# Head outputs placed transposed by transfers, inverse of the sums on ScalarE, product on GpSimd

## The chip, the core and the metric

The kernel runs on one core of a Trainium2 chip. The metric is device time in microseconds, the median of several executions. The engines are TensorE (PE, with its weight loads as PEld), VectorE (DVE), ScalarE (ACT), GpSimd (POOL) and SyncE (SP), which here only issues transfers. Each engine works off its own queue in the order written; semaphores tie the queues together.

## What is computed

Two decoder layers over x, 16 batches of 256 tokens and 256 channels in float32, with a context of the same shape. Every sublayer is followed by a normalisation without parameters:

```python
x = _layernorm(x + _L0_attn_ref(x, ...))            # 16 heads of 16, rope
x = _layernorm(x + _L0_xattn_ref(x, ctx, ctx, ...)) # gated linear mixing, 8 heads of 32
x = _layernorm(x + _L0_ffn_ref(x, ...))             # quantised, relu^2 * up
x = _layernorm(x + _L1_attn_ref(x, ...))            # 16 heads of 16
x = _layernorm(x + _L1_xattn_ref(x, ctx, ctx, ...)) # 16 heads of 16, keys from ctx
x = _layernorm(x + _L1_ffn_ref(x, ...))
```

In the three attentions with 16 heads, which are all that matters here:

```python
attn = softmax(q @ k.T / 4)            # 256 x 256 for each head
out = attn @ v                         # 256 x 16 for each head, the heads side by side
return out @ w_proj + b_proj
```

## The kernel before

**Lanes.** Four batches are in work at a time, one in each lane, and each lane does four batches one after the other (`it` 0 to 3). A lane has its own tiles: XO (the stream and a second half, `outputs`), YX (two halves: Y, and XT_ which is also OT), QK, V, PB, U. `lane_steps` lists the steps of one batch, `PARTS` says which engines take part in each. `TURNS` holds for each engine a string of digits: the lane whose next step that engine takes. This is a merge of the four lanes, written out by hand or by a planner, and it is the order of each queue. `PLACES` gives each use of psum its first bank of eight.

**One attention.** The steps are xT (transpose of the stream), qk (projection, split into two halves of 16 bits, written to DRAM by SyncE), stack (read back with head pairs on partitions), v, then eight steps max (scores of one pair of heads on TensorE L767, row maxima on VectorE L1170), negmax (the maxima as a further row of Q), eight steps exp (scores again L786, exponential on ScalarE L1005) and between them four steps pv.

**From pv to proj.** A pv step (L804) multiplies with weights of 32 columns out of V. V keeps for each head 16 values and a column of ones, 17 columns side by side, so that a head's 32 rows in psum hold 16 numerators, the sum of the exponentials, and rows that nobody needs. ScalarE copies psum to U in two pieces of 128 x 512 (L1009). The step heads turns U by eight transposes into two psum banks (L817), VectorE takes the reciprocal of the 32 sums of each token (L1181) and multiplies into `outputs` (L1183). The step oT turns this back by four transposes (L681, through `turn_x`), ScalarE copies to OT (L1012), and proj multiplies OT by W_o (L694, through `tokens_out`). VectorE then adds the stream (L1189), and moments and norm follow (L1100, L1103, L958, L960, L1111). GpSimd has the rope sums (L1342), the bias for the stream (L1347) and two products in mixout (L1357, L1361).

**Order around it.** K of the third attention is projected and stored while the second runs: its copy on ScalarE goes into U and so waits for `o_ready` of the second (L985). `loadx` waits for oT of the third attention (L638). The first heads step of each batch waits for the store of the batch before, which reads the same half of XO (L1180).

Of the kernel before, what the change touches and what calls it, by code (L numbers as in the profile page):

```python
# [12 lines left out]
ALU = mybir.AluOpType  # L13
# [3 lines left out]
P = 128  # L17
LANES = 4
# [10 lines left out]
SLOT = 32  # L29
# [15 lines left out]
    "exp": "pe act", "pv": "pe act", "heads": "pe dve", "oT": "pe act", "proj": "pe dve act", "norm": "dve",  # L45
# [7 lines left out]
WIDTH = {"ctx": 1, "xT": 1, "rope": 1, "qk": 1, "v": 1, "max": 2, "negmax": 1, "exp": 2, "pv": 1, "heads": 2, "oT": 1,  # L53
# [4 lines left out]
def lane_steps():  # L58
# [6 lines left out]
    def attention(a):  # L65
# [15 lines left out]
        add("pv", a, 3)  # L81
        add("heads", a)
# [4 lines left out]
        add("oT", a)  # L87
# [57 lines left out]
def lane_program(lane):  # L145
# [7 lines left out]
    for at in range(-1, batches):  # L153
# [10 lines left out]
        "0010002102210131223113433220000000000011011110010100322001203202101202211103111230103112020133000001"  # L164
        "2001003102202213213222121321111120331120110021200233301332330222223322032230101321131100021103030310"
        "1013333302322103323320300120230100012011001021120032332133001130321230110212112312121332132111132332"
        "1322233212213222302300022220331323330032031211033311310001332223301223002002021021103223011201221211"
        "0212021323213330200000120200101200001333211130010331211113003332303322300311032113200323112223111230"
        "0002100120133100230320301110333011210211103331120212203012001033122002310102212022133201133223121123"
        "1112333210330130320331023300322022322303010121112203223010201203130003301331121232033233220031000231"  # L170
        "0000120011011100001202111232033031113111321123221322111122313330210001202233302220322303220233200122"
        "2201123001002033210030133310333103123202230333301113000032220311101121021130012220122210222010123231"
        "1212123031211110332111320023000223301333312333122033122300230103200230101230100132220130111030331021"
        "1011233330000322133211301002100120012230322032213231331222321211132123301000231102033323302102212313"
        "3201303032322220320120030031313331331100103310232312211210032320002010010100110111000020232333021330"
        "1121321112311221110231022111120013022300220122102223223320002222111200100030211323300110301320211210"
        "3111233130233310000033211333122312333130130013030022002221322322111223311233011121033212300111203320"
        "0323330222331233311222031112030110000320003002230303033303332033331220211312201112011231000110031032"
        "1031001220332221022133122223121111123311211023101002203303332033320223222131101310221322101232330103"
        "0131033313020200023232033221003230001000102110012011220130331331100130321131121221312232213111131023"  # L180
        "3032132212233232223022013211022223133112333113332100233113011033332213110112011232100231000021002012"
        "0033202210220322223022312333121321233301333203332330323032321320233330330"),
    "act": (
        "0012000311242211332000000000301003011011110110121010221000002010122201022122220311111120331022021233"
        "3003333122210233221300101321130123213311123333221033203002200300300200023230231203011330110310111113"
        "3131211312221222122122232222333332332320333300033310000003121113002320121221102212211022100200000120"
        "0200110123111133211133333332232313120103022233230000002203310030301111033013101110331110002300122122"
        "1012102221211220021311023333023033120332330031221202230101302112033211221333312311221033220030002000"
        "0002033000123110123203203111111131313111333132112222222220222022020300200203320330033033313303033310"
        "1130000130311111211001222022212220012102211112121112112232323313332333303220300023220000330200310311"  # L190
        "0130313011011303030011331310020122220122021201122221130211303202330112332003322203313013100322132322"
        "1303213331312313021212111030223000030000000023022302330132011113111131113111123212231222012222232000"
        "2220002000220001011113110333301130300003311333132313313300300122022212222021112112111231122333212333"
        "2223333320230000003220003020320033333003333310111011103111100110020122120221202122120232111103311203"
        "1202103213303320333122232101032120110323123320131323311222330220300020030023000032221303130110331011"
        "1111331133111320102122122222222322223333323332133231131333111113011131003000010002001202221220222022"
        "122311113303322333333330032232202310203333330"),
    "dve": (
        "0012210004321344311220000000044111111141223223202220033300330010031010033011020112112002210121201121"
        "3200013100232120100302302123013123321313132112313132010233000223232202223323111333131333130002022012"  # L200
        "0200112111113222332232223300330333120012200001033030001110000011113212213312112111222122030302203333"
        "2202231300331130011330333010120100212010221010321113003211220000321230002010222111332332113121113103"
        "1203030302223032222213232211133310000103330030333312211222112111022220303333222302003011100030320332"
        "1121330111300000011112212231223113211222200022033033222333001300133103033033113201002210022101201113"
        "0002131232102000233021332100202113321123321131111110312330002220330222322302021211001031000331332221"
        "1121231313231130322202022223313330031100000330333301112331020021110001012112121123112332220003332332"
        "2320223022330033130013130033101101200112210101212112020311223030122132300102023213000020213312312311"
        "3113131302203302023223222220331311133133013333001102122111211200200333223023222132213130330033332221"
        "33311222333000"),
    "pool": (  # L210
        "0022211033030032110112210320113332230000110302223111220330012231313102122003331122333010022000111102"
        "22300113330113322221003203311313022000211111122003232223330001112030023213133332233110122203"),
    "sp": (
        "4220011300002121110224443313332443000011110221223333201100011322202313233001200000312110111222223133"
# [92 lines left out]
def decoder_kernel(nc, x, ctx, consts, w_qkv0, w_proj0, w_gates, b_gates, w_gate, w_up, w_down,  # L307
# [3 lines left out]
    with es:  # L311
# [167 lines left out]
        def freed_by(it, name, L, occ, unit, j):  # L479
# [22 lines left out]
            if name == "heads":  # L502
                return [(o_ready[L], a + 1)]
# [896 lines left out]
```

## Time and profile before

| what | value |
|---|---|
| median of 3 runs | 1617.05 us (1615.44 to 1617.6) |
| profiled execution, its own time | 1622.2 us |
| its span | 1620.4 us |
| busy: PE, DVE, ACT, POOL | 1465.2, 1183.2, 950.7, 225.4 us |
| granted TensorE clock, mean | 0.969 |
| largest group on DVE | row maxima, 384 x 1223 ns |
| largest group on ACT | exponentials, 384 x about 1025 ns |

Busy time of an engine is the union of its instructions. TensorE's matmuls are pipelined, so the duration of one (some 280 to 400 ns) is longer than the pace at which they follow each other. Idle time of an engine is put down to what ended it.

### The profile page before, as it was taken

What the parts mean: (1) busy time and instruction counts of PE and PEld (TensorE: products, weight loads), DVE (VectorE), ACT (ScalarE), POOL (GpSimd) and SP (SyncE); (2) the same over time, 40 slices, a digit from 0 to 9 for tenths busy, and PEclk for the clock granted to TensorE, in tenths of its full rate; (3) what the DMA queues carried; (4) which work ended last, traced back from release to release, by engine and by line L of the source; (5) the groups of instructions that cost most, each with busy time, mean ns of one, the idle gap of its engine ahead of it and who ended that gap; (6) DMA issues with size and microseconds to landing.
All of it is one profiled execution on the core that took longest, in us unless ns stands there. A gap on an engine that the chain in (4) does not pass through costs nothing. (4 is left out here: it accounts for less than half of the span.)

```text
span 1620.4 us, 31692 instructions
## 1 busy us (share of the span) xinstructions
PE 1465.2 (90%) x12482; PEld 972.9 (60%) x12482; DVE 1183.2 (73%) x2103; ACT 950.7 (59%) x1701; POOL 225.4 (14%) x233
## 2 busy tenths in 40 slices
PE   7588799899999879899999888998999988898998
PEld 4155556557766556557767555565776656465577
DVE  5978887865568888974765888866565788888632
ACT  3378466674466757566355666656545586655752
POOL 6011100002221011002212210000122111100100
PEclk9699989999999999999999898999999999999999
DMA  8430113322121021521321011331322101133200
GB/s 273 139 102 2 52 47 105 118 60 79 53 69 51 2 63 48 152 67 58 119 73 53 1 47 33 93 108 50 111 72 66 53 2 46 47 97 110 70 1 26
DMA packets 115074, 114.34 MB, mean 71 GB/s; under 512 B 9842, under 2 KB 100722, under 8 KB 114930
## 3 DMA queue, kind: packets, MB, share of 16 engines
q1 hardware_dynamic: 114610, 111.28, 22.4%
q8 instruction: 102, 1.67, 0.4%
q10 hardware_dynamic: 320, 1.05, 0.3%
q14 instruction: 42, 0.34, 0.1%
HBM read 68.91 MB, written 42.99 MB: 69 GB/s over the span
## 5 line engine op out<-in xcount | busy, mean ns | idle before, releaser
L1170 DVE TENSOR_REDUCE nm<-psum 128x4 f16<-128x1024 f32 x384 | 455.1, 1223 | 100.3 <-PE psum L767 99.2
L1005 ACT ACTIVATE PB<-psum 128x1024 f32<-128x1024 f32 x288 | 288.3, 1024 | 87.1 <-PE psum L786 85.7
L804 PE MATMUL psum<-PB,V 128*32 128x256 f32 x2304 | 206.8, 390 | 7.4 <-ACT PB L1005 5.2
L1347 POOL TENSOR_TENSOR XO<-XO,row_b 128x512 f32<-128x512 f32 x80 | 103.2, 1300 | 749.8 <-ACT YX L976 749.8
L767 PE MATMUL psum<-QK 48*128 48x256 f16 x1536 | 140.4, 280 | 46.8 <-DVE nm L1170 22.7
L786 PE MATMUL psum<-QK 49*128 49x256 f16 x1536 | 138.3, 277 | 21.4 <-ACT PB L1005 5.3
L767 PEld LDWEIGHTS psum<-QK 48*128 48x128 f16 x1536 | 58.9, 96 | 109.8 <-DVE nm L1170 38.8
L786 PEld LDWEIGHTS psum<-QK 49*128 49x128 f16 x1536 | 54.2, 95 | 111.4 <-issue 42.1
L930 PE MATMUL psum<-YX,W 128*128 128x256 f32 x512 | 120.0, 385 | 0.0
L804 PEld LDWEIGHTS psum<-PB,V 128*32 128x32 f32 x2304 | 79.9, 110 | 62.6 <-issue 20.0
L938 PE MATMUL psum<-W,PB 128*128 128x256 f32 x512 | 116.3, 382 | 0.0
L1005 ACT ACTIVATE YX<-psum 128x1024 f32<-128x1024 f32 x96 | 98.7, 1028 | 20.3 <-PE psum L786 20.0
L804 PE MATMUL psum<-YX,V 128*32 128x256 f32 x768 | 101.3, 385 | 5.1 <-ACT PB L1005 4.9
L930 PEld LDWEIGHTS psum<-YX,W 128*128 128x128 f32 x512 | 94.4, 190 | 17.3 <-issue 4.2
L938 PEld LDWEIGHTS psum<-W,PB 128*128 128x128 f32 x512 | 95.8, 190 | 13.9 <-issue 1.7
L694 PE MATMUL psum<-W_o,YX 128*128 128x256 f32 x384 | 97.8, 401 | 1.1 <-ACT YX L1012 0.5
L1111 DVE TENSOR_SCALAR XO<-YX,mv,rstd 128x256 f32<-128x256 f32 x192 | 79.5, 457 | 24.6 <-ACT rstd L960 24.3
L1009 ACT ACTIVATE U<-psum 128x512 f32<-128x512 f32 x112 | 66.9, 599 | 50.6 <-PE psum L804 43.3
L681 PE MATMUL psum<-cst,XO 128*128 128x128 f32 x512 | 81.8, 283 | 13.3 <-DMA XO<-in_x 4.2
L694 PEld LDWEIGHTS psum<-W_o,YX 128*128 128x128 f32 x384 | 73.1, 199 | 16.1 <-issue 2.6
L681 PEld LDWEIGHTS psum<-cst,XO 128*128 128x128 f32 x512 | 58.4, 142 | 38.9 <-issue 16.3
L1189 DVE TENSOR_TENSOR YX<-psum,XO 128x512 f32<-128x512 f32 x48 | 33.0, 688 | 64.3 <-PE psum L694 44.4
(171 smaller groups left out, 2675.4 us busy)
## 6 DMA issues: line engine op xcount, KB each, us to landing
QK<-heads_dram SPq DMA_DIRECT2D x96, 512.0 KB, 3.8
heads_dram<-U SPq DMA_DIRECT2D x288, 128.0 KB, 2.0
XO<-in_x SPq DMA_DIRECT2D x16, 256.0 KB, 3.2
YX<-in_ctx SPq DMA_DIRECT2D x16, 256.0 KB, 3.4
out<-XO SPq DMA_DIRECT2D x16, 256.0 KB, 2.5
W<-in_w SPq DMA_DIRECT2D x2, 1024.0 KB, 6.9
heads_dram<-PB ACTq DMA_DIRECT2D x4, 256.0 KB, 9.4
W_gu<-in_w_down SPq DMA_DIRECT2D x1, 1024.0 KB, 5.6
```

The lines of the kernel that those rows point to most:

```text
L681: ins = pe.transpose(bank[:, k * TOK + t * P:k * TOK + t * P + P], src[:, t, k * P:(k + 1) * P], ident)
L694: ins = pe.matmul(bank[:, t * DIM:(t + 1) * DIM], xt(k)[:, t * P:(t + 1) * P], w[:, k], start=(k == 0), stop=(k == n - 1))
L767: ins = pe.matmul(b[:, e * 512 + t * TOK:e * 512 + (t + 1) * TOK], QS[L][r, unit, t * P:(t + 1) * P], KS[L][r, unit, :], start=True, stop= ...
L786: ins = pe.matmul(b[:, e * 512 + t * TOK:e * 512 + (t + 1) * TOK], KS[L][r, unit, t * P:(t + 1) * P], QS[L][r, unit, :], start=True, stop= ...
L804: ins = pe.matmul(b[SLOT * j:SLOT * j + SLOT, at:at + TOK], value(L, t, PAIRS * e + u, HEADS, HD, SLOT), src, start=(t == 0), stop=(t == T ...
L930: ins = pe.matmul(b[:, m * TOK:(m + 1) * TOK], W_1[:, k, c:c + P], XT_[L][:, k, :], start=(k == 0), stop=(k == KT - 1))
L938: ins = pe.matmul(b[:, 0:DIM], hid1(L, k)[:, unit * P:(unit + 1) * P], W_2[:, k], start=(k == 0), stop=(k == IT - 1))
L1005: act.activation(weights_of(L, unit), b[:, 0:1024], ACT.Exp, scale=HD ** -0.5)\
L1009: act.activation(flat2(U[L][:, unit - 1:unit + 1, :]), b[:, 0:512], ACT.Copy).then_inc(u_ready[L], 1)
L1111: dve.tensor_scalar(stream(L, it)[:, t], Y[L][:, t], mv[L][:, t, 0:1], rstd[L][:, t:t + 1], ALU.subtract, ALU.mult).then_inc(x_ready[L], 1)
L1170: dve.tensor_reduce(nm[L][:, :, :, unit].rearrange("p t e -> p e t"), b[:, 0:1024].rearrange("p (e t k) -> p e t k", e=2, t=TT), AX.X, ALU ...
L1347: pool.tensor_tensor(stream(L, it), stream(L, it), row_b[:, occ:occ + 1, :].to_broadcast([P, TT, DIM]), ALU.add).then_inc(xb_ready[L], 1)
```

## The change

V becomes `[P, 1024]`: each head has 32 columns in which value and one alternate, so numerators come on even rows and copies of the sum on odd rows, 16 of each a head. The steps heads (of TensorE and VectorE) and oT disappear. A new step spread issues four transfers on SyncE after the second copy to U: even rows of two groups of U to OT, odd rows to `sums`, which is the Y half of YX, each transfer 64 partitions by 2 x 256. The step heads is now Ln and Exp with scale -1 on ScalarE over `sums`, in place, and a product of OT and `sums` in place on GpSimd. Then proj, as before.

```diff
-    "exp": "pe act", "pv": "pe act", "heads": "pe dve", "oT": "pe act", "proj": "pe dve act", "norm": "dve",
+    "exp": "pe act", "pv": "pe act", "spread": "sp", "heads": "act pool", "proj": "pe dve act", "norm": "dve",
...
-        V = lanes("V", [P, TT * HEADS * (HD + 1) + SLOT])
+        V = lanes("V", [P, TT * HEADS * 2 * HD])
...
+        sums = [v[:, 0].rearrange("p (k t) -> p k t", k=KT) for v in YX]
+        VA, ones = ([v[:, :].rearrange("p (n d c) -> p n d c", d=HD, c=2)[:, :, :, n] for v in V] for n in range(2))
...
+        def value(lane, t, e, u):
+            at = (t * HEADS + PAIRS * e + u) * 2 * HD
+            return V[lane][:, at:at + 2 * HD]
...
                 elif name == "loadx" and it:
-                    sp.wait_ge(turned[L], nth(TURNED, it - 1, "oT2"))
+                    sp.wait_ge(turned[L], nth(TURNED, it - 1, "quant"))
...
+                elif name == "spread":
+                    sp.wait_ge(u_ready[L], it * U_USES + U_AT[occ] + 2)
+                    for home, other in ((OT, 0), (sums, 1)):
+                        for g in range(2):
+                            sp.dma_start(home[L][64 * g:64 * g + 64, :, :], U[L][other:P:2, g:4:2, :])\
+                              .then_inc(spread[L], 16)
...
-                elif name == "oT":
-                    b = claim(*step)
-                    pe.wait_ge(o_ready[L], it * ATTN + occ + 1)
-                    filled(turn_x(outputs(L, it), b), *step)
                 elif name == "proj":
...
-                    pe.wait_ge(turned[L], nth(TURNED, it, f"oT{occ}"))
+                    pe.wait_ge(o_ready[L], it * ATTN + occ + 1)
...
                         if unit:
-                            act.wait_ge(o_ready[L], it * ATTN + 2)
+                            act.wait_ge(spread[L], (it * ATTN + 2) * 64)
...
-                elif name == "oT":
-                    b = wait_full(act, *step)
-                    act.activation(flat2(OT[L][:, :, :]), b[:, 0:512], ACT.Copy).then_inc(turned[L], 1)
+                elif name == "heads":
+                    act.wait_ge(spread[L], (it * ATTN + occ + 1) * 64)
+                    log = own(act.activation(flat2(sums[L][:, :, :]), flat2(sums[L][:, :, :]), ACT.Ln))
+                    wait_own(log)
+                    act.activation(flat2(sums[L][:, :, :]), flat2(sums[L][:, :, :]), ACT.Exp, scale=-1.0)\
+                       .then_inc(inverse_ready[L], 1)
...
-                    inverse = own(dve.reciprocal(sums, b[:, :, HD]))
-                    wait_own(inverse)
-                    dve.tensor_tensor(outputs(L, it).rearrange("p t (h d) -> p (t h) d", d=HD), b[:, :, 0:HD],
-                                      sums.rearrange("p (h d) -> p h d", d=1).to_broadcast([P, TT * HEADS, HD]),
-                                      ALU.mult).then_inc(o_ready[L], 1)
...
+                elif name == "heads":
+                    pool.wait_ge(inverse_ready[L], it * ATTN + occ + 1)
+                    pool.tensor_tensor(flat2(OT[L][:, :, :]), flat2(OT[L][:, :, :]), flat2(sums[L][:, :, :]), ALU.mult)\
+                        .then_inc(o_ready[L], 1)
```

The wait for the store of the batch before moves to mixnorm on ScalarE, the first writer of `outputs` that is left. The memsets of V become memsets of its columns of ones, once a lane at the start, and half of them again before the second attention. The small tiles aT, eneg, den, vr, q_s, h_s and q_k share one tile. `TURNS` and `PLACES` are new throughout: TensorE has 1777 steps in place of 1873, ScalarE 1345 as before, VectorE 966 (1014), GpSimd 240 (192), SyncE 342 (294).

## Rows read from the trace of the kernel before

**Rows 1.** The page, busy time of each engine, share of the span, instructions.
```profile
PE 1465.2 (90%) x12482; PEld 972.9 (60%) x12482; DVE 1183.2 (73%) x2103; ACT 950.7 (59%) x1701; POOL 225.4 (14%) x233
```
**Rows 2.** Stretches of 100 us: length, busy of each engine, clock, transfers.
```profile
core 0: us, PE busy (x) PEld busy (x) DVE busy (x) ACT busy (x) POOL busy (x), PEclk, DMA share, GB/s
...
400.00:500.00 100.00, 99.28 (x759) 69.72 (x757) 61.14 (x99) 53.83 (x98) 19.93 (x18) 1.00 0.23 71
500.00:600.00 100.00, 83.54 (x777) 52.85 (x776) 87.05 (x180) 66.38 (x136) 12.79 (x13) 0.93 0.06 20
...
900.00:1000.00 100.00, 83.98 (x706) 53.77 (x704) 84.23 (x176) 61.57 (x133) 16.23 (x16) 0.88 0.07 20
```
**Rows 3.** Who waited for whom: us in total, times, longest.
```profile
PEld psum L767 <- DVE nm L1170: 38.8, 53, 5.4
...
PEld psum L804 <- ACT PB L1005: 23.9, 48, 1.2
...
PEld psum L786 <- ACT PB L1005: 21.3, 42, 1.6
...
PEld psum L767 <- ACT PB L1005: 12.0, 22, 2.1
```
**Rows 4.** Groups by line and form: count, busy us, mean ns, idle before, releaser.
```profile
L681 PE MATMUL psum<-cst,XO 128*128 128x128 f32 x512 | 81.8, 283 | 13.3 <-DMA XO<-in_x 4.2 <-DVE XO L1183 3.9 <-DVE XO L1111 2.7
...
L817 PE MATMUL psum<-cst,U 128*128 128x128 f32 x448 | 61.7, 279 | 3.8 <-DVE nm L1170 1.8 <-ACT U L1009 1.4 <-ACT YX L976 0.3
...
L1183 DVE TENSOR_TENSOR XO<-psum,rs 128x512 f32<-128x512 f32 x48 | 33.2, 691 | 1.7
...
L1012 ACT ACTIVATE YX<-psum 128x512 f32<-128x512 f32 x48 | 28.7, 600 | 40.0 <-PE psum L681 39.9
...
L1181 DVE RECIPROCAL rs<-psum 128x32 f32<-128x32 f32 x48 | 16.9, 352 | 41.1 <-PE psum L817 40.9
```
**Rows 5.** Instructions in order of time, 1570 to 1577 us: start, us.
```profile
1570.69 1.07 PE L804 MATMUL psum<-PB,V 128*32 128x256 f32 x16
...
1573.53 1.04 PE L817 MATMUL psum<-cst,U 128*128 128x128 f32 x8
...
1574.40 1.89 PE L930 MATMUL psum<-YX,W 128*128 128x256 f32 x8
...
1576.13 0.60 PE L681 MATMUL psum<-cst,XO 128*128 128x128 f32 x4
...
1576.56 1.89 PE L930 MATMUL psum<-YX,W 128*128 128x256 f32 x8
```
**Rows 6.** Instructions on heads_dram: ns to issue (min/median/max), then landing of 128 KB.
```profile
L644 SPq DMA_DIRECT2D heads_dram<-U x192: 354/470/3081, 21.6 to 1522.9; - x192
...
DMA to landing us min/median/max: 1.8/2.1/12.0
```
**Rows 7.** Landing of the 512 KB reads of line L653; the page's queue line.
```profile
DMA to landing us min/median/max: 3.1/3.8/6.7
...
q1 hardware_dynamic: 114610, 111.28, 22.4%
```
**Rows 8.** Groups by line and form, for the prices of added instructions.
```profile
L1347 POOL TENSOR_TENSOR XO<-XO,row_b 128x512 f32<-128x512 f32 x80 | 103.2, 1300 | 749.8 <-ACT YX L976 749.8
...
L1009 ACT ACTIVATE U<-psum 128x512 f32<-128x512 f32 x112 | 66.9, 599 | 50.6 <-PE psum L804 43.3 <-PE psum L887 6.8
...
L1072 ACT ACTIVATE PB<-PB 128x1024 f32<-128x1024 f32 x32 | 33.8, 1057 | 1.0
```
**Rows 9.** VectorE and GpSimd in order of time near 555 us; line L1111, ns.
```profile
554.65 2.93 DVE L1111 TENSOR_SCALAR XO<-YX,mv,rstd 128x256 f32<-128x256 f32 x2
...
554.71 1.26 POOL L1357 TENSOR_TENSOR XO<-YX,row_b 128x512 f32<-128x512 f32 x1 [15.03 <-DVE YX L1256]
556.10 1.26 POOL L1361 TENSOR_TENSOR YX<-XO 128x512 f32<-128x512 f32 x1
...
L1111 DVE TENSOR_SCALAR XO<-YX,mv,rstd x192: 380/407/1564, 90.9 to 1617.4; 128x256 f32<-128x256 f32 x192
```
**Rows 10.** Groups by line and form, for the prices of TensorE's steps.
```profile
L767 PE MATMUL psum<-QK 48*128 48x256 f16 x1536 | 140.4, 280 | 46.8 <-DVE nm L1170 22.7 <-DVE U L1153 6.6 <-DMA QK<-heads_dram 5.5
...
L938 PE MATMUL psum<-W,PB 128*128 128x256 f32 x512 | 116.3, 382 | 0.0
```

More of the change, by code:

```diff
@@ L51 @@
 }
-WIDTH = {"ctx": 1, "xT": 1, "rope": 1, "qk": 1, "v": 1, "max": 2, "negmax": 1, "exp": 2, "pv": 1, "heads": 2, "oT": 1,
+WIDTH = {"ctx": 1, "xT": 1, "rope": 1, "qk": 1, "v": 1, "max": 2, "negmax": 1, "exp": 2, "pv": 1,
          "proj": 1, "gates": 1, "vm": 1, "turn": 1, "decay": 2, "mix": 2, "mixv": 1, "mixnorm": 1, "quant": 1, "gate": 2, "up": 2,
@@ L81, in attention @@
         add("pv", a, 3)
+        add("spread", a)
         add("heads", a)
@@ L238 @@
+    "03536036153560526043642604306406310474163452707505227610615425024"
 )
@@ L373, in decoder_kernel @@
         nmT = [v[64:64 + HEADS, 0:TOK // 2].bitcast(F16) for v in GN]
-        rs = lanes("rs", [P, TT, HEADS])
         st = lanes("st", [P, TT, 6])
@@ L379, in decoder_kernel @@
         M3 = lanes("M3", [P, TOK], BF16)
-        aT = lanes("aT", [P, TT, MH])
-        eneg = lanes("eneg", [P, TT, MH])
-        den = lanes("den", [P, TT * MH])
-        vr = lanes("vr", [P, TT * MH])
-        q_s = lanes("q_s", [P, TT, 4])
-        h_s = lanes("h_s", [P, TT, 6])
-        q_k = lanes("q_k", [P, TT, 3])
+        small = lanes("small", [P, 4, TT * MH])
+        aT, eneg = ([v[:, n].rearrange("p (t h) -> p t h", t=TT) for v in small] for n in range(2))
+        den, vr = ([v[:, n] for v in small] for n in (2, 3))
+        q_s, h_s, q_k = ([v[:, 0:2].rearrange("p n c -> p (n c)")[:, at:at + TT * n].rearrange("p (t n) -> p t n", t=TT) for v in small]
+                         for at, n in ((0, 4), (8, 6), (20, 3)))
         heads_dram = [nc.dram_tensor(f"heads_dram{i}", [2, 2, 4, HD, PAIRS, TOK], F16, kind="Internal").ap()
@@ L406, in decoder_kernel @@
         o_ready, y_ready, moments, x_ready = (lane_sem(n) for n in ("o_ready", "y_ready", "moments", "x_ready"))
+        spread, inverse_ready = lane_sem("spread"), lane_sem("inverse_ready")
         mix_dve, quantized = lane_sem("mix_dve"), lane_sem("quantized")
@@ L458, in weights_of @@
             return YX[lane][:, :, :].rearrange("p a n -> p (a n)") if u % SLOTS == PBUF else PB[lane][:, u % SLOTS, :]
-        def value(lane, t, h, heads, width, columns):
-            at = (t * heads + h) * (width + 1)
-            return V[lane][:, at:at + columns]
+        def value(lane, t, e, u):
+            at = (t * HEADS + PAIRS * e + u) * 2 * HD
+            return V[lane][:, at:at + 2 * HD]
         def decays(lane, h, n):
@@ L501, in freed_by @@
                 return [(u_ready[L], it * U_USES + U_AT[occ] + unit // 2 + 1)]
-            if name == "heads":
-                return [(o_ready[L], a + 1)]
-            if name == "oT":
-                return [(turned[L], nth(TURNED, it, f"oT{occ}"))]
             if name == "proj":
@@ L1322, in _ @@
             for L in range(LANES):
-                setup(pool.memset(V[L][:, :], 0.0))
-            pool.wait_ge(set_pool, 4 + LANES)
-            for L in range(LANES):
-                setup(pool.memset(VA[L][:, :, :, HD:HD + 1], 1.0))
+                setup(pool.memset(ones[L], 1.0))
             setup(pool.memset(ones_sq, 1.0))
```

171 lines of the change are left out of this document (81 added, 90 removed).

## The prediction

> **What bounds the kernel now.** I read the busy shares first, then the table by stretches of 100 us, then who waits for whom. TensorE is busy 1465.2 us of 1620.4, VectorE 1183.2, ScalarE 950.7, GpSimd 225.4 [rows 1]. A share of 90% is an average: in six of the sixteen stretches TensorE is busy 94 to 99 us of 100 (300 to 500, 700 to 900, 1100 to 1300), and nothing but its own work can shorten these. In 0 to 200, 500 to 600, 900 to 1000 and 1300 to 1400 it is at 66 to 87 while VectorE mostly stands at 84 to 90 [rows 2]: there the row maxima set the pace. The waits say the same: TensorE's weight loads wait for the maxima to free a bank (38.8 us) and for the exponentials of ScalarE (23.9, 21.3 and 12.0 us) [rows 3]. So: TensorE first, VectorE second, ScalarE in short waits. The granted clock is 1.00 in the full stretches and 0.88 to 0.93 in the two thin ones shown, both far nearer the 2.4 GHz level than 1.2.
>
> **What the change removes.** There are 48 attentions (16 batches, 3 each). Each loses eight transposes of U (step heads), one reciprocal and one 128x512 product on VectorE, four transposes (step oT) and one 128x512 copy on ScalarE. TensorE: the transposes of U are 448 instructions in 61.7 us, of which 384 belong to attentions: 52.9 us; those of XO are 512 in 81.8 us, 192 of them oT: 30.7 us; together 83.6 us [rows 4]. This is the upper bound, since a group's busy time holds a modelled tail that overlaps the next group. The lower bound comes from starts: eight transposes begin at 1573.53 and the next matmuls at 1574.40, four begin at 1576.13 and the next at 1576.56, so 0.87 + 0.43 = 1.30 us an attention, 62.4 us in all [rows 5]. I take the middle, 73 us. VectorE loses 16.9 + 33.2 = 50.1 us, ScalarE 28.7 us [rows 4]. The two psum banks of heads and one of oT are also no longer claimed; no wait names them alone, so nothing is booked.
>
> **What it adds.** The weighted sums keep their 32 columns, now values and ones alternating, so their matmuls cost the same. SyncE issues four transfers of 128 KB, ScalarE runs Ln and Exp over 128x512 in SBUF, GpSimd one 128x512 product. A transfer of 128 KB takes 0.47 us to issue and lands 2.1 us after its issue [rows 6]; one of 512 KB lands in 3.8 [rows 7]. An activation over 1024 SBUF columns takes 1.057 us and one over 512 from psum 0.599, so I price each of the two at 0.60; the nearest GpSimd product takes 1.30 on average [rows 8], and 1.26 undisturbed [rows 9]. ScalarE: 48 x 1.20 - 28.7 = +28.9 us; GpSimd +62 us, on an engine 14% busy; transfers +25 MB on a queue that holds the 16 DMA engines for 22.4% of the span with 111 MB [rows 7]: +5 points. SyncE: 192 more issues, 90 us, on a queue that mostly waits; behind a spread step stand most often a qk step (20 of 48) and a negmax (8), which it can hold for its 1.9 us of issuing, or longer when the last pair of U is late.
>
> **Where it lies.** The new chain from the last weighted sum to proj is 0.60 (copy to U) + 4 x 0.47 + 2.1 (last landing) + 1.20 + 1.27 + six hand-overs of about 0.1 = 7.65 us. The old one was 0.60 + 0.87 + 0.36 + 0.69 + 0.43 + 0.60 + 0.6 = 4.2 us. So each attention takes 3.5 us longer in its lane, and the question is whether TensorE's written order covers it, because its queue stops at proj until o_ready. I expanded the new order: between the last pv step and proj of the same attention stand 4 to 20 steps of other work, 11.3 on average (before, 5 to 19 and 11.5, of which two were heads and oT). Priced by step (a max or exp step 140.4 / 384 = 0.37 us, a down1 step 116.3 / 32 = 3.6 [rows 10], a pv step 1.07 and a projection about 1.9 [rows 5], and so on) and stretched so that the whole order fills 1565 us, these gaps are 5.5 us at least and 9.3 in the middle. Eight of the 48 are under 7.65, short by 4.5 us together. If the chain were 10 us, 31 would be short by 49 us; at 12 us 36 by 118. The same limit stands for ScalarE: it waits for the transfers at the head of its queue with exp steps behind it (in the new order 13 times at once), and its U copy of another lane too.
>
> **The sum.** Relief of TensorE 73. Charged back: (a) in 5 of 16 stretches VectorE sets the pace and its relief is 50, so (73 - 50) x 5/16 = 7; (b) late proj steps 4.5; (c) VectorE and GpSimd disturb each other. Beside two GpSimd products a pair of normalising instructions took 2.93 us [rows 9], where one such takes 0.380 at least and two 0.73. There are 96 such pairs; a further 48 products with a window of 2.0 us each meet 96 x 48 x 2.0 / 1570 = 6 of them at some 1.2 us: 7 us with both sides' delays, bounds 0 and 61 (every product holds VectorE for its 1.27 us); (d) ScalarE goes from 58.7% to 62% busy, so its queueing (share over the rest) grows by a sixth, and the 57.2 us that loads wait for it [rows 3] by 10. Total 28.5; gain 44.5. The profiled execution took 1622.2 us, its span 1620.4: 1622.2 - 44.5 = 1577.7. The median of the runs, 1617.05, lies 5.15 below, so 1572.5; I say 1572. The new merges and bank places were drawn up afresh for all engines: no row prices that; the nearest is TensorE's idle 155 us, of which a tenth either way, 15 us, goes into the range and nothing into the value. The start and the end: the first memsets and the last down1 steps keep their kind and count; 0.
>
> On (c), the Trainium skill (SBUF — State Buffer, Who interferes with whom) says that a VectorE instruction with two SBUF inputs, or in a two-port mode, and a GpSimd instruction that reads SBUF lock each other out for a whole instruction. By that rule the trace agrees in kind [rows 9], and by it the change moves work into the lock.
>
> On the transfers, the Trainium skill (DMA: Bandwidth & Descriptors, Rules for kernel authors) says of two transfers to disjoint halves of the partitions that they serialize, since both use all 16 DMA engines, and advises one; here there are four of 64 partitions. By that, four times 2.1 us would make a chain of about 12 us. The trace speaks against it so far: of 288 transfers of 128 KB, issued in twos and threes less than half a microsecond apart, the median lands in 2.1 us [rows 6].
>
> **Rivals.** (1) *The relief counts only where TensorE is full.* Elsewhere it turns into longer waits for the maxima and for lanes that got 3.5 us longer. Then 6/16 x 73 = 27 less charges of about 10: 1617 - 17 = 1600. For it: the waits [rows 3]. Against: VectorE is relieved by 50 too. (2) *The upper bound holds*: 83.6 and hardly a charge, the longer chain wholly under other lanes' work: 1535. For it: gaps of 9.3 against 7.65. (3) *Slower: the transfers land late.* The place is the proj step at the head of TensorE's queue. It decides from a chain of 10 us, a last landing of 4.5 us in place of 2.1, since the 49 us short then eat the gain. At 12 us, 118 - 4.5 = 113.5; half of it is won back because the other lanes are then readier: 1572 + 57 = 1629. For it: landings up to 12.0 and 6.7 us [rows 6, 7], and stacks of 512 KB in the same stretches. Against: the medians. (4) *The lock holds VectorE for every product*: 61 instead of 7: 1626. Against: most VectorE time is maxima with one psum input. (5) *No effect within 0.2%*: the charges meet the relief, 1617.
>
> **How the numbers follow.** Forecast, 1550 to 1592: 0.56. Rival 1: 0.17. Rival 2: 0.10. Rival 3: 0.09. Rival 4: 0.03. Rival 5: 0.05. Faster by over 0.2% (below 1613.8) 0.56 + 0.17 + 0.10 = 0.83; within 0.2%, about what a measurement of this kernel tells from no change, 0.05; slower 0.12. The range: below, relief 83.6 with no charge and a few us of better merging, 1530; above, rival 1 with its own spread, 1607. Left out are rivals 3 to 5 and the edges, just under 0.2.
>
> **What the profile after would show.** TensorE near 1390 us busy with 576 transposes fewer and idle near 185; VectorE about 1133 to 1140; ScalarE about 980; GpSimd near 287; the four transfers landing at 2 to 2.5 us; waits of the proj matmuls for GpSimd under 10 us; normalising pairs beside GpSimd products in some 15 places. Wrong would be: landings over 4.5 us, proj waits of tens of us, idle time of TensorE grown by more than 60 us (then rival 1 or 3), a ScalarE activation from SBUF over 0.7 us, or a TensorE clock well under the 0.97 of the span.

## The result and the profile after

The changed kernel takes 1661.7 us in the median (1656.4 to 1667.6), beside 1617.3 us for the kernel before (1615.4 to 1620.0): a ratio of 1.027 [1.023, 1.031]. It is slower by 44 us where 45 faster was forecast, and 55 us above the end of the range. The profiled execution has a span of 1662.0 us and a mean granted clock of 0.949, against 1620.4 and 0.969 before.

The busy line of the page, which answers to [rows 1]:

```profile
PE 1438.5 (87%) x11886; PEld 930.7 (56%) x11906; DVE 1139.1 (69%) x2007; ACT 979.4 (59%) x1749; POOL 288.5 (17%) x277
```

All three helpers came out as forecast (VectorE 1133 to 1140, ScalarE 980, GpSimd 287). TensorE did not (near 1390 was forecast): its 576 transposes are gone, yet it is busy only 27 us less, and its idle time (span less busy) rose from 155 to 223 us. So the time came as idle time of TensorE. A part of the small 27 is the clock: busy time times granted clock is 1420 before and 1365 after, 55 us less work, and the lower clock stretches what is left. (That product is a fair measure of TensorE's work here: four more kernels below run the same 12482 instructions as the kernel before, and it is 1418 to 1421 for them.)

Who waited for whom, from all of the run (engine, line, what it waited for: us, times, longest), which answers to [rows 3]:

```profile
ACT YX L1006 <- DMA YX<-U: 96.0, 41, 5.5
...
PEld psum L767 <- DVE nm L1172: 38.3, 52, 3.0
...
PEld psum L786 <- ACT PB L999: 26.5, 38, 2.2
...
PEld psum L804 <- ACT PB L999: 25.1, 40, 1.6
...
PEld psum L694 <- issue: 22.5, 39, 2.5
...
PE psum L694 <- POOL YX L1331: 19.6, 15, 3.1
```

The old waits stand nearly where they stood. New are the first and the last: ScalarE stands at Ln for the transfers in 41 of 48 attentions, 96 us in all, and TensorE stands at proj (L694) for GpSimd's product. The weight loads of proj wait 22.5 us where they waited 4.9 before. From the single instructions, proj starts within 0.2 us of the end of the product in 19 of 48 attentions.

One attention in order of time (start us, us, engine, line, operation, tiles; in brackets the idle time before it and what ended it):

```profile
1145.99 0.60 ACT L1003 ACTIVATE U<-psum 128x512 f32<-128x512 f32 x1 [1.19 <-PE psum L804]
...
1146.62 3.32 SPq L653 DMA_DIRECT2D YX<-U  x4
...
1152.63 0.63 ACT L1006 ACTIVATE YX<-YX 128x512 f32<-128x512 f32 x1 [1.89 <-DMA YX<-U]
...
1153.29 0.63 ACT L1008 ACTIVATE YX<-YX 128x512 f32<-128x512 f32 x1
...
1153.83 1.01 ACT L999 ACTIVATE PB<-psum 128x1024 f32<-128x1024 f32 x1
1154.00 1.26 POOL L1331 TENSOR_TENSOR YX<-YX 128x512 f32<-128x512 f32 x1 [2.43 <-ACT YX L1008]
...
1155.38 2.07 PEld L694 LDWEIGHTS psum<-W_o,YX 128*128 128x128 f32 x8 [2.07 <-issue]
1155.41 2.76 PE L694 MATMUL psum<-W_o,YX 128*128 128x256 f32 x8 [1.82 <-POOL YX L1331]
```

Here the whole mechanism stands in a few lines. The copy to U begins at 1145.99 and the product ends at 1155.26, 9.3 us later; ScalarE stands idle for 1.89 us with an exp (1153.83) behind it, TensorE for 1.82 us with other lanes' steps behind proj. Over the 48 attentions that stretch, from the start of the last U copy to the end of the product, is 8.7 us at least and 8.9 in the middle; the prediction said 7.65.

The rows of the transfers (ns to issue, least/median/most; then the landing), which answer to [rows 6]:

```profile
L653 SPq DMA_DIRECT2D YX<-U x192: 593/607/2047, 76.0 to 1624.2; - x192
...
DMA to landing us min/median/max: 2.9/3.4/4.6
```

Groups by line, which answer to [rows 8]:

```profile
L1331 POOL TENSOR_TENSOR YX<-YX 128x512 f32<-128x512 f32 x48 | 62.0, 1291 | 668.9 <-ACT YX L1008 668.8
...
L1006 ACT ACTIVATE YX<-YX 128x512 f32<-128x512 f32 x48 | 30.2, 630 | 96.0 <-DMA YX<-U 96.0
```

And the three stretches of [rows 2] (columns as there):

```profile
400.00:500.00 100.00, 93.56 (x701) 63.98 (x694) 60.03 (x94) 51.05 (x90) 24.76 (x22) 1.00 0.28 75
500.00:600.00 100.00, 81.52 (x788) 50.81 (x787) 82.53 (x158) 70.75 (x143) 16.16 (x14) 0.95 0.18 51
900.00:1000.00 100.00, 86.83 (x816) 53.82 (x818) 78.94 (x164) 73.38 (x147) 13.42 (x13) 0.95 0.20 54
```

The stretch that was full, 99.28 us of 100, now has holes, though with the whole kernel running late it no longer holds quite the same work. That is the opposite of relief.

### The profile page after: what moved, and what is told of

It is laid out like the page before. It is cut to its first block and busy times, and to the rows that moved or that the text cites. A ratio compares the mean times of both kernels' runs of the same rounds, so it can differ in the third digit from the quotient of the medians.

```text
span 1662.0 us, 30607 instructions
## 1 busy us (share of the span) xinstructions
PE 1438.5 (87%) x11886; PEld 930.7 (56%) x11906; DVE 1139.1 (69%) x2007; ACT 979.4 (59%) x1749; POOL 288.5 (17%) x277
## 2 busy tenths in 40 slices
DMA packets 142719, 139.46 MB, mean 84 GB/s; under 512 B 12914, under 2 KB 128370, under 8 KB 142578
## 5 line engine op out<-in xcount | busy, mean ns | idle before, releaser
L999 ACT ACTIVATE PB<-psum 128x1024 f32<-128x1024 f32 x288 | 287.7, 1024 | 103.5 <-PE psum L786 102.3
L804 PE MATMUL psum<-PB,V 128*32 128x256 f32 x2304 | 214.8, 403 | 14.5 <-ACT PB L999 9.9
L1331 POOL TENSOR_TENSOR YX<-YX 128x512 f32<-128x512 f32 x48 | 62.0, 1291 | 668.9 <-ACT YX L1008 668.8
L786 PE MATMUL psum<-QK 49*128 49x256 f16 x1536 | 143.4, 283 | 33.7 <-ACT PB L999 13.4
L694 PE MATMUL psum<-W_o,YX 128*128 128x256 f32 x384 | 106.6, 426 | 23.8 <-POOL YX L1331 19.6
L804 PE MATMUL psum<-YX,V 128*32 128x256 f32 x768 | 104.8, 395 | 4.0 <-ACT PB L999 4.0
L694 PEld LDWEIGHTS psum<-W_o,YX 128*128 128x128 f32 x384 | 77.5, 211 | 43.2 <-issue 16.1
L1006 ACT ACTIVATE YX<-YX 128x512 f32<-128x512 f32 x48 | 30.2, 630 | 96.0 <-DMA YX<-U 96.0
```

The costliest lines, as they stand in the source:

```text
L694: ins = pe.matmul(bank[:, t * DIM:(t + 1) * DIM], xt(k)[:, t * P:(t + 1) * P], w[:, k], start=(k == 0), stop=(k == n - 1))
L786: ins = pe.matmul(b[:, e * 512 + t * TOK:e * 512 + (t + 1) * TOK], KS[L][r, unit, t * P:(t + 1) * P], QS[L][r, unit, :], start=True, stop= ...
L804: ins = pe.matmul(b[SLOT * j:SLOT * j + SLOT, at:at + TOK], value(L, t, e, u), src, start=(t == 0), stop=(t == TT - 1))
L999: act.activation(weights_of(L, unit), b[:, 0:1024], ACT.Exp, scale=HD ** -0.5)\
L1331: pool.tensor_tensor(flat2(OT[L][:, :, :]), flat2(OT[L][:, :, :]), flat2(sums[L][:, :, :]), ALU.mult)\
```

## The experiments

Times are medians beside the kernel before on the same chip; where two experiments are compared, I take the difference of their ratios times 1617. The theory from the profile after: the transfers make the chain longer than the new orders allow, and each late proj is passed on to every queue. Against it: the order is at fault, ScalarE's stall, or the lock of VectorE.

**old_order: the new flow in the old order.** The orders of before with heads and oT struck, and the new steps put in their places.

> The new data flow (transfers, inverse on ScalarE, product on GpSimd) in the old merge: the order and bank places of the kernel before, with heads and oT struck out of TensorE's and VectorE's queues, ScalarE's new step where oT stood, spread and the GpSimd product put in where the trace of before has their inputs ready. Theory T1 (the chain from the last weighted sums to proj is 8.9 us instead of 7.65 and stalls TensorE at proj): the old order leaves less other work in that gap than the new one, so it is no faster than the changed kernel, 1660 to 1720 us. Theory T2 (the newly drawn merge and bank places cost what the relief gives): 1560 to 1590 us.

Measured: 1795.3 us, ratio 1.109 [1.105, 1.113]. That is slower than the 1660 to 1720 expected. Two waits at proj (L699), and two of ScalarE for the transfers, in all of the run:

```profile
PEld psum L699 <- issue: 99.3, 44, 8.5
...
PE psum L699 <- POOL YX L1336: 95.0, 38, 8.3
...
ACT U L987 <- DMA YX<-U: 60.0, 14, 6.1
...
ACT YX L1011 <- DMA YX<-U: 49.4, 18, 5.9
```

The place of the wait is proj, as the theory says. But the kernel differs from the changed one in two more ways. ScalarE's new step stands in oT's place, a choice of mine. And the copy of K for the third attention (L987) now stands ahead of that step and waits for the transfers itself, 60 us in all, where the changed kernel waits at Ln alone. So the 176 us are no measure of the old order itself.

**no_transfer: what the transfers cost.** SyncE issues none; ScalarE copies U to both homes.

```diff
-  ... sp.dma_start(home[L][64*g:64*g+64, :, :], U[L][other:P:2, g:4:2, :])
-  log = own(act.activation(flat2(sums...), flat2(sums...), ACT.Ln))
-  act.activation(flat2(sums...), flat2(sums...), ACT.Exp, scale=-1.0)
+  log = own(act.activation(flat2(sums...), flat2(U[L][:, 2:4, :]), ACT.Copy))
+  act.activation(flat2(OT...), flat2(U[L][:, 0:2, :]), ACT.Copy)
```

> The changed kernel without its 192 transfers: ScalarE copies two groups of U to sums and two to OT (two instructions of 128x512, as many as Ln and Exp), so the product works on unplaced data. Left out: the placing and the inverse. The chain loses 4 issues and the landing, 5.5 of 8.9 us. T1: TensorE's idle 224 us falls by 60 or more, 1570 to 1600 us. T2: the order is unchanged, so 1640 to 1660 us.

Measured: 1608.3 us, 0.993 [0.990, 0.995]. Without transfers the change is a small gain; 56 us of loss come with them. But even so the gain is 12 us, not 44: part of the forecast fell for another reason.

**old_no_transfer: the same in the old order.**

> The new data flow without transfers (two copies of 128x512 on ScalarE in their place, the copies of the second attention taken from CT; the placing and the inverse are left out) in the order and bank places of the kernel before, less heads and oT. Beside no_transfer (1608 us, the same flow in the new order) it is the price of the order. If the new order is worth less than the old one once the chain is short, this one is at 1550 to 1575 us. If the removed transposes are simply worth little (the time is held by VectorE, the lanes and the clock), it is within 10 us of 1608.

Measured: 1689.5 us, 1.042 [1.039, 1.045]. Neither of the two outcomes expected came. It is again far above its twin in the new order, again with ScalarE's step in oT's place. The transfers cost 108 us in the old order and 56 in the new. That the new order absorbs a part of them is likely but not shown: some of the 108 are the waits of K's copy.

**sums_first: only the sums hold up ScalarE.** The sums' two transfers are issued first and have their own semaphore; GpSimd waits for the numerators. It computes the same as the changed kernel.

```diff
-  for home, other in ((OT, 0), (sums, 1)):
+  for home, other, done in ((sums, 1, spread_sums), (OT, 0, spread)):
...
-  act.wait_ge(spread[L], (it * ATTN + occ + 1) * 64)
+  act.wait_ge(spread_sums[L], (it * ATTN + occ + 1) * 32)
...
+  pool.wait_ge(spread[L], (it * ATTN + occ + 1) * 32)
```

> The changed kernel with the two transfers of the sums issued first and counted on a semaphore of their own, so that Ln and Exp run while the numerators land: the chain is 1.3 us shorter, all work is the same. T1: 48 late steps of which about 18 are late by it: 10 to 30 us faster than the changed kernel, 1632 to 1652 us. T2: within 5 us of it.

Measured: 1617.7 us, 0.999 [0.997, 1.001]. The waits that changed:

```profile
ACT YX L1006 <- DMA YX<-U: 41.6, 23, 3.9
...
PE psum L693 <- POOL YX L1332: 5.5, 8, 1.5
```

Ln and Exp now run beside the numerators' landing. The chain falls from 8.9 to 7.8 us in the middle (from 8.7 to 7.4 at least), and the whole loss goes: 46 us for 1.1 to 1.3 us of chain in 48 attentions, twice what was expected.

**whole_rows: the step in the source.** The source is 64 neighbouring partitions instead of every second one; bytes, packets and issues are the same.

```diff
-  U[L][other:P:2, g:4:2, :]
+  U[L][64 * other:64 * other + 64, g:4:2, :]
```

> The changed kernel with each transfer taking 64 neighbouring rows of U in place of every second row, same bytes and packets; Ln and Exp are copies here, since numerators land in sums. Left out: the right placing and the inverse. If the step of two rows is what makes a landing 3.5 us instead of 2.1, it falls to 2.1 and the time by 15 to 30 us. If the landing is set by four transfers of 64 partitions one behind another, it stays at 3.3 to 3.5 and the time within 5 us of the changed kernel.

Measured: 1629.4 us, 1.006 [1.004, 1.008]. Its transfers:

```profile
L653 SPq DMA_DIRECT2D YX<-U x192: 590/609/1886, 78.7 to 1597.6; - x192
...
DMA to landing us min/median/max: 2.4/2.4/4.1
```

The landing is 2.4 us in place of 3.4, the issue as before, and the kernel gains 35 us. Each of the four, issued 0.6 us apart, lands after 2.4 us, so they don't stretch one another here; with the step the first takes 3.0 in the middle and the last 3.5. What makes 3.4 is which partitions are read: every second one of 128, not 64 neighbours. Ln and Exp are copies in this kernel, but they take 0.630 us each as before.

**first_and_whole: both.**

> sums_first and whole_rows together: sums issued first with their own semaphore, each transfer from 64 neighbouring rows (landing 2.4 us instead of 3.5); Ln and Exp are copies, the placing and the inverse are left out. The chain is 6.4 us, against 7.5 in sums_first, 7.7 in whole_rows and 3.3 in no_transfer. If the gain saturates once the chain is under the gaps of the written order: 1606 to 1614, as without any transfer. If each microsecond of chain is worth the same throughout: about 1590.

Measured: 1609.2 us, 0.994 [0.991, 0.996]: as no_transfer, though all the transfers are there. Their load on the DMA engines costs nothing that can be told from the noise here (2 us, with intervals of 4 either way); what costs is their latency.

The chain of all these, and of the next two experiments, with least and median over the 48 attentions, worked out from single instructions of the traces (start of the last U copy to the end of the product; in the kernel before, to the end of the copy to OT):

| kernel | least | median | ratio |
|---|---|---|---|
| kernel before | 4.3 | 7.2 | 1 |
| no_transfer | 3.2 | 7.2 | 0.993 |
| act_free | 7.1 | 7.3 | 0.996 |
| first_and_whole | 6.4 | 7.6 | 0.994 |
| sums_first | 7.4 | 7.8 | 0.999 |
| whole_rows | 7.6 | 8.4 | 1.006 |
| tuned | 7.4 | 8.4 | 1.014 |
| changed kernel | 8.7 | 8.9 | 1.027 |

Down to a median of 7.6 or so a shorter chain is worth something; below it ScalarE isn't at the step yet (median 7.2 where 3.2 would do), and nothing more comes. The first row matters as much. The old chain could take 4.3 us, but in the middle it took 7.2, because its steps stood in the queues waiting for their turn. So up to about 7.2 us the new chain replaces waiting that was there already, and only the rest is late.

**act_free: is it ScalarE's stall?** ScalarE does five small activations in place of Ln and Exp and never waits for the transfers; GpSimd does.

```diff
-  act.wait_ge(spread[L], ...)
-  ... Ln, Exp
+  for n in range(5): ... act.activation(spare, ident[:, 0:16], ACT.Copy)
...
-  pool.wait_ge(inverse_ready[L], ...)
+  pool.wait_ge(spread[L], ...)
```

> The changed kernel with ScalarE not waiting for the transfers: in its step heads it runs five small copies on a spare tile (about 1.2 us as before), and GpSimd multiplies as soon as the transfers have landed. Left out: the inverse. The chain is 1.3 us shorter, as in sums_first (1617 us), but ScalarE's 96 us of waiting at that step are gone wholly, where sums_first keeps 42. If only the length of the chain counts: 1612 to 1622. If ScalarE's stall with exponentials queued behind it is a cause of its own: 1595 to 1610.

Measured: 1615.7 us, 0.996 [0.993, 0.999], overlapping sums_first. With ScalarE's wait at this step wholly gone, the gain over sums_first is 5 us, within the noise, and no more than the still shorter chain (7.3 for 7.8 us) would give. The stall acts as a part of the chain; a cost of its own doesn't show.

**tuned: ScalarE's step later.** sums_first, with ScalarE's step moved one to three steps back in 14 places, behind steps of other lanes, and proj in 4.

> sums_first with 15 or so of ScalarE's heads steps moved behind one to three steps of other lanes, where they waited over 0.5 us for the transfers, and five proj steps moved behind one step of TensorE. Same work. If ScalarE's stalls are a cause: 5 to 15 us faster than sums_first, 1603 to 1612. If not: within 4 us of it, or slower since the inverse comes later.

Measured: 1642.9 us, 1.014 [1.008, 1.020], 25 us worse than sums_first. Moving the wait away from the head of ScalarE's queue moves the inverse, and with it proj, later: the chain is 8.4 us in the middle for 7.8. Here such local moves did harm even though the moved step had waited.

**struck_old and struck_new: what the removed work is worth.** In both, heads and oT are struck with their transposes, the reciprocal and the product, and ScalarE copies U to OT once; one stands in the old order, one in the new.

```diff
-  "heads": "pe dve", "oT": "pe act"
+  "oT": "act"
...
-  b = wait_full(act, *step)
-  act.activation(flat2(OT...), b[:, 0:512], ACT.Copy)
+  act.wait_ge(u_ready[L], ...)
+  act.activation(flat2(OT...), flat2(U[L][:, 0:2, :]), ACT.Copy)
```

> The kernel before, in its own order and bank places, with heads struck out (eight transposes, reciprocal, product) and the four transposes of oT: in oT's place ScalarE copies 128x512 from U (from CT in the second attention) to OT. Left out: placing and normalising. No wait is later than before, and 576 transposes, 50 us of VectorE and all three hand-overs are gone. It is the purest price of what the change removes. By the sum of the prediction (73 of TensorE, nothing charged back): 1545 to 1565 us. If the removed work hardly sets the pace (rival 1 at its hardest): 1590 to 1615 us.

> The changed kernel in its new order without transfers, inverse and product: ScalarE copies 128x512 from U to OT in its step heads and releases proj. Left out: placing and normalising. Beside no_transfer (1608 us) it lacks 30 us of ScalarE, 62 us of GpSimd and 1.9 us of chain. Beside struck_old it is the price of the newly drawn order at equal work. If the two orders are equally good: within 10 us of struck_old. If the new order is the poorer one by itself: 20 to 50 us slower than struck_old; if the better one, faster.

Measured: 1602.4 us, 0.990 [0.988, 0.992], and 1598.2 us, 0.987 [0.984, 0.989]. The busy line of struck_old, span 1599.3:

```profile
PE 1411.4 (88%) x11906; PEld 913.9 (57%) x11906; DVE 1136.2 (71%) x2007; ACT 950.8 (59%) x1701; POOL 225.5 (14%) x233
```

TensorE is busy 54 us less (62 less by busy time times clock, 1358 for 1420) and its idle time is 33 us more: three fifths of what was taken out turn into holes. All that the change removes is worth 16 us in the old order and 22 in the new. The two orders differ by some 5 us, and their intervals overlap.

**before_longer: a longer chain in the kernel before.** GpSimd squares OT between oT and proj; TensorE's work and order are untouched. GpSimd's own order isn't quite: the new products are put between its other steps, some of which move.

```diff
-  pe.wait_ge(turned[L], nth(TURNED, it, f"oT{occ}"))
+  pe.wait_ge(late_ready[L], it * ATTN + occ + 1)
...
+  pool.wait_ge(turned[L], nth(TURNED, it, f"oT{occ}"))
+  pool.tensor_tensor(flat2(OT...), flat2(OT...), flat2(OT...), ALU.mult).then_inc(late_ready[L], 1)
```

> The kernel before with one product of GpSimd on OT (a square, so the numbers are not the reference's) between ScalarE's copy and proj: the chain from the last weighted sums to proj is 1.35 us longer, nothing else. If the slope found in the changed kernel (44 us for 1.3 us) holds for any order drawn up tightly around a chain: 1640 to 1665 us. If the old order has slack there, as the 2 us of other steps between oT and proj suggest: 1620 to 1635 us.

Measured: 1674.6 us, 1.035 [1.031, 1.040]: 57 us. The chain is longer by less than the 1.35 us expected in most places, since the square takes 1.04 us: from the end of the copy to OT to the end of the product it is 1.12 to 1.20 us in 41 of 48 attentions, and 1.6 to 10.9 in seven, where the product comes late. The sum is 76 us, of which the 57 are three quarters. The busy line and the product's, from an execution of 1686.8 us, the slowest of the four:

```profile
PE 1491.3 (89%) x12482; PEld 984.8 (58%) x12482; DVE 1188.1 (71%) x2103; ACT 951.4 (56%) x1701; POOL 274.9 (16%) x281
...
L1351 POOL TENSOR_TENSOR YX<-YX 128x512 f32<-128x512 f32 x48 | 50.1, 1044 | 608.8 <-ACT YX L1018 608.8
```

Its wait at proj (L700), which the kernel before has nowhere:

```profile
PE psum L700 <- POOL YX L1351: 39.8, 37, 7.8
```

The kernel before has little slack at this place either. The same 12482 instructions of TensorE took 1491 us in place of 1465, at a granted clock of 0.953 for 0.969. But the clock isn't the main cost: the fastest of the four runs took 1670.9 us at 0.967, where the kernel before beside it took 1614.7 to 1622.3 at 0.965 to 0.975.

**with_transposes and in_place: busy time or place?** Both are struck_old with 12 dummy transposes an attention put back on TensorE: in with_transposes just ahead of proj, in in_place eight where heads stood and four where oT stood.

```diff
+  for n in range(12): pe.transpose(b[:, P*(n%4):P*(n%4)+P], ident, ident)   # proj
...
+  for n in range(8 if name == "heads" else 4): ins = pe.transpose(...)      # heads, oT
```

> struck_old (1602 us) with twelve transposes of the constant identity put back on TensorE ahead of each proj, into the bank that proj then overwrites: 576 transposes and some 62 to 75 us of TensorE are there again, while VectorE's reciprocal and product and the hand-overs stay out. Left out as in struck_old: placing and normalising. If TensorE's occupancy sets the pace, as the prediction took it: the time rises by 40 us or more, above 1640. If the order is paced by chains through several engines and the 16.5 us of struck_old are what TensorE's time is worth: 1612 to 1620. If the 16.5 us came from VectorE or the hand-overs: within 4 us of 1602.

> struck_old (1602 us) with the twelve transposes of the identity an attention put back where heads (8) and oT (4) stood in the old order, in their old banks, waiting for nothing. TensorE does as much as before and as in with_transposes (1653 us, all twelve ahead of proj); VectorE's work and the hand-overs stay out. Left out: placing and normalising. If the transposes stood in slots of the order in which TensorE had to wait anyway, so that the place decides and not the busy time: 1605 to 1620. If busy time counts wherever it stands: 1645 to 1660.

Measured: 1652.9 us, 1.023 [1.020, 1.025], and 1612.0 us, 0.995 [0.993, 0.998]. Their busy lines, spans 1649.4 and 1611.4:

```profile
PE 1464.4 (89%) x12482; PEld 975.6 (59%) x12482; DVE 1137.6 (69%) x2007; ACT 949.4 (58%) x1701; POOL 225.4 (14%) x233
```

```profile
PE 1463.8 (91%) x12482; PEld 971.7 (60%) x12482; DVE 1135.9 (70%) x2007; ACT 951.3 (59%) x1701; POOL 225.7 (14%) x233
```

The busy times are equal within 0.6 us, the cost is 53 us in one and 9 in the other. This is the cleanest of the pairs: the same 53 us of TensorE work cost 1.1 us an attention directly ahead of proj, 0.2 where it had stood. TensorE's idle time says how: 188 us in struck_old, 185 in with_transposes, 148 in in_place. Where they had stood, the transposes fill 40 us of holes; directly ahead of proj they fill 3. (in_place also claims the old banks again, with_transposes doesn't; what that is worth wasn't separated.)

**small_product: VectorE's relief alone.** In the kernel before, the product over 128x512 becomes one over 128x32.

> The kernel before with VectorE's product of 128x512 in the step heads made a product of 128x32, and the four transposes of oT taking CT: all of TensorE's work is there, VectorE has 25 us less and the chain is 0.5 us shorter. The product is left out. If VectorE's relief sets the pace: 8 to 20 us faster than before, 1597 to 1609. If not: within 5 us of 1617.

Measured: 1621.6 us, 1.001 [0.999, 1.004]. VectorE is busy 1162.6 us in place of 1183.2, the chain is 3.8 us at least in place of 4.3 but 7.1 for 7.2 in the middle, and nothing comes of either.

## Why the prediction was wrong

**The ladder.** From the ratios, times 1617: all that is removed, in the new order, -22; ScalarE's second instruction and GpSimd's product (no_transfer less struck_new) +10; the transfers with neighbouring rows and sums first +2, less than the intervals tell from nothing; the step of two partitions +8; waiting for all four before Ln +46. Together +44. The last two depend on the order in which they are taken: with whole_rows as the rung between, waiting for all four is +19 and the step +35. It is the length of both together that tells, 54 us.

**Where the 89 us lie.** The forecast of 1572.5 us missed the measured 1661.7 by 89. Without the transfers the gain was 12 us where 44.5 was forecast, which is 33 of them; the transfers, by what they add to the chain, are the other 56, where 4.5 had been charged for late proj steps.

**The relief, 73 us, is the first step that failed.** The count of instructions and their 62 to 84 us of TensorE were right: struck_old is busy 54 us less at a clock of 0.962 for 0.969, or 62 of the same clock, which is the prediction's lower bound. But its price was read as busy time, and TensorE's written order fixes what comes behind a removed step: if that step's data or bank isn't ready, a hole stays. Worth 16 to 22 us with VectorE's 50 us of relief included. Rival 1 had this mechanism and left 27 of the 73. in_place confirms it from the other side (9 us for putting them back), and up to 350 us struck_old is nowhere ahead of the kernel before (0 to 3 us behind, by its exponentials); its whole gain builds up behind that. Charge (a) goes with it: in 5 of 16 stretches VectorE's relief was to set the pace, at 50 us for an entire run, and in the first of them nothing came; of 21 us less in VectorE's product, small_product got nothing.

**The chain, 7.65 us, was mis-sized.** By medians over the 48 attentions: the issues 1.96 us up to the start of the last one (1.88 was booked; 0.607 each in place of 0.470, but the last is hidden in the landing), the last landing 3.5 in place of 2.1, Ln and Exp 1.29 in place of 1.20, the product 1.27 as booked, all hand-overs together some 0.15 in place of 0.6. The sum is 8.8 us, and the landing is the term that was off. The row used for the landing, [rows 6], is a write to HBM (and its 2.1 is the median over all transfers of heads_dram, the reads of 512 KB among them; the writes alone land in 2.0), and this is a copy inside SBUF with a step: whole_rows shows 2.4 us for the copy and 1.0 for the step. The old chain was mis-read too: 4.2 us is its least (4.3 in the trace), but as it ran it took 7.2 in the middle, so in the middle the change made it 1.7 us longer, not 3.5. The Trainium skill's rule (DMA: Bandwidth & Descriptors, Rules for kernel authors) on transfers to disjoint halves says that they serialize, and the prediction made a chain of about 12 us of it. That isn't what is seen: the chain is 8.9 us, and the four transfers of whole_rows, issued 0.6 us apart, land 2.4 us after their issue each. Their landings overlap; whether the data of one waits for that of another within those 0.6 us, no run tests.

**The price of lateness is the largest failure.** Between its entries for 7.65 us (4.5 short) and 10 us (49 short), the prediction's table gives 4.5 + (8.9 - 7.65) / 2.35 x 44.5 = 28 us short at 8.9, and rival 3 was to decide from 10 us, with half won back. The changed kernel lost 46 us between 7.8 and 8.9. The likely reason, argued from the queues and not isolated by a run: the table counted the gap of each attention by itself, in an average pace, on TensorE's queue alone. But lateness at proj is hardly absorbed by the next gap. All other lanes' steps queue behind it on TensorE, and through them on ScalarE and VectorE; those of the waiting lane queue in turn. The traces show that it builds up over the run: between sums_first and the changed kernel the same exponential is 10 us later at 390 us, 24 at 810, 31 at 1300 and 46 at the end, with no single jump, but with next to nothing added from 810 to 1120. Three kinds of lengthening, in the old and the new order, cost alike: 76 us of GpSimd in 48 places 57 us, 1.1 us of transposes (53 / 48) 53, 1.1 to 1.3 us of landing 46, that is 0.7 to 1.0 of the length in all 48. (The transposes are TensorE's own work ahead of proj and not a wait there.) So rival 3 named the outcome and its cause, late transfers at proj. But it was to decide from 10 us and a last landing of 4.5, and half was to be won back, which gave 1629. It decided from about 7.5 us and a last landing of 3.5, and little was won back.

**What held.** The waits named as signs of rival 3 came: TensorE's idle time grew by 68 us (over 60 was the mark), the waits at proj by 20 us for the product and 18 for the weight loads. The landings stayed under the mark of 4.5 us but for the longest, 4.6: that mark was set too high. The busy times of the three helpers were within 2 us. Charge (c) was small: 20 of the normalising instructions overlap a GpSimd instruction after, 18 before, some 10 us more than undisturbed in both. Charge (d), ScalarE's queueing, 10 us, is near the +10 of no_transfer, which holds a longer chain too, and these two weren't separated. Charge (b) was the right place with the wrong price.

**What stays open.** Old and new order differ by 5 us for the struck flow, within the noise; how much a merge drawn for a chain of 8.9 us would win back wasn't tried. The clock is the smaller part of the +46: sums_first took 1620.0 us in a run with a granted clock of 0.951, the changed kernel 1659.5 in one with 0.951, so some 40 us stand at an equal clock. No kernel here with the new flow in full beats the kernel before; sums_first equals it.

## What to carry to other kernels

In a kernel whose queues follow a written order, price a change by the longest chain of the lane, not by the busy time of the busiest engine. Measure that chain as it runs, with its waits for a turn, not as the sum of its instructions. Up to the length it has in the middle a new chain cost nothing here; beyond it, 0.7 to 1.0 of every microsecond came back in every pass. Before a transposition on TensorE is replaced by transfers, add issue, landing, and the instructions behind the landing, take the landing from a transfer of the same kind (both ends and the step), and ask which instruction needs which of them: letting the sums go first was worth 46 us here, with no work less. To learn what a removal is worth, strike it and run that.

## What the runs showed of the hardware

- A copy inside SBUF of 64 partitions, 2 KB each, lands 3.4 us after its issue when the source takes every second partition and 2.4 us when it takes neighbours (2.9 and 2.4 at least), with the same packets and bytes (142719 packets, 139.46 MB in both kernels).
- Such a copy holds SyncE's issue for 0.607 us; a write of the same 128 KB to HBM 0.470 [rows 6].
- ScalarE takes 0.630 us for 128x512 from SBUF to SBUF and 0.595 to 0.600 from psum.
- GpSimd takes 1.04 us for the square of a 128x512 tile and 1.27 for a product of two (before_longer and the changed kernel).
- The mean granted clock was lower in most kernels with more idle time of TensorE: 0.969 before (155 us idle), 0.953 with a longer chain (194, and 0.967 in the fastest run of the same kernel), 0.949 in the changed kernel (223), 0.924 in the old order with transfers (316). But with_transposes has 185 us idle, is 2% slower than before and stands at 0.970: loss and clock needn't go together.
- TensorE's busy time times its granted clock is 1418 to 1421 us in five kernels with the same 12482 instructions, at clocks of 0.953 to 0.970.
